# The middle stretch of an attention kernel: its 256-column score step first of four instead of third

## What is computed

```python
xn = _layer_norm(x, ln_g, ln_b)                     # x: (4, 1024, 128)
q, k, v = (xn @ w + b).reshape(B, S, 16, 64).transpose(0, 2, 1, 3)
scores = jnp.einsum('bhqd,bhkd->bhqk', q, k) / jnp.sqrt(jnp.float32(64))
mask = jnp.tril(jnp.ones((S, S), bool), k=-1)
scores = jnp.where(mask, NEG_INF, scores)
a = jax.nn.softmax(scores, axis=-1)
h = jnp.einsum('bhqk,bhkd->bhqd', a, v)
return h.transpose(0, 2, 1, 3).reshape(B, S, 1024) @ w0 + b0 + residual
# then: router on the first tokens, 8 experts of rank 16, top 2, layer norm, residual
```

## Time and profile before

| what | us |
|---|---|
| three runs | 1078.06 (median), 1075.38, 1082.80 |
| the profiled execution's own time | 1075.12 |
| its span, first to last instruction | 1073.4 |
| PE busy | 999.1, 93% |
| POOL busy | 703.0, 65% |
| DVE busy | 584.1, 54% |
| ACT busy | 536.4, 50% |

### The profile page before, as it was taken

One profiled execution on the slowest core, in us unless ns is written; L12 is line 12 of the kernel. 1 busy time (PEld: TensorE's weight loads), 2 busy tenths in 40 slices (PEclk: granted clock), 3 DMA queues, 4 the chain that ended last, 5 costly groups with the idle time before them and its releaser, 6 DMA issues.

```text
span 1073.4 us, 23006 instructions
## 1 busy us (share of the span) xinstructions
PE 999.1 (93%) x9557; PEld 643.1 (60%) x9557; DVE 584.1 (54%) x996; ACT 536.4 (50%) x735; POOL 703.0 (65%) x503
## 2 busy tenths in 40 slices
PE   3699999999999999999999999999999999999972
PEld 2465666666666665666666566666666666666542
DVE  5655554554456556455646656545554555545354
ACT  4244545554444554654455464555355445454343
POOL 6077666667766767785667768666568766666652
PEclk9899999999999999999999999999999999999995
DMA  3000010001101100002010201010100200100101
GB/s 106 20 2 22 21 22 18 6 22 41 22 22 41 22 3 21 22 22 42 21 21 3 61 21 22 22 22 19 25 22 22 61 22 22 22 3 21 22 22 39
DMA packets 61816, 27.11 MB, mean 25 GB/s; under 512 B 39056, under 2 KB 53776, under 8 KB 61712
## 3 DMA queue, kind: packets, MB, share of 16 engines
q1 hardware_dynamic: 61712, 25.64, 10.3%
HBM read 22.76 MB, written 2.35 MB: 23 GB/s over the span
## 4 chain that ended last, share of the span: by engine, by line
PE 81%; DVE 8%; ACT 8%; issue 2%; POOL 1%; DMA 0%; POOLq 0%; ACTq 0%
PE both L614 23%; PE st L599 15%; PE s_ps L560 8%; PE st L653 5%; PE st L594 5%; DVE least L987 4%; PE st L526 4%; ACT ring L835 3%; PE st L588 3%; ACT total L835 3%; PE both L624 3%; PE st L528 3%; PE st L527 3%; PE s_ps L564 2%; PE st L542 2%
## 5 line engine op out<-in xcount | busy, mean ns | idle before, releaser
L407 POOL TENSOR_TENSOR total<-total,ring 128x1024 f32<-128x1024 f32 (+1 forms) x315 | 543.4, 1725 | 317.0 <-PE both L614 268.7
L987 DVE TENSOR_REDUCE least<-s_ps 128x2 f32<-128x1024 f32 x315 | 313.0, 1011 | 280.0 <-PE s_ps L564 185.9
L835 ACT ACTIVATE ring<-st 128x1024 f32<-128x1024 f32 (+1 forms) x256 | 233.7, 918 | 207.2 <-PE st L599 206.8
L614 PE MATMUL both<-ring,v_sb 128*64 128x512 f32 (+3 forms) x1280 | 210.7, 467 | 0.0
L599 PE MATMUL st<-q_high,k_low 64*128 64x512 f32 (+3 forms) x768 | 172.6, 446 | 0.0
L614 PEld LDWEIGHTS both<-ring,v_sb 128*64 128x64 f32 x1280 | 89.0, 137 | 132.9 <-issue 122.9
L560 PE MATMUL s_ps<-k_high,q_high 64*128 64x512 f32 (+1 forms) x758 | 147.6, 402 | 17.5 <-DVE least L987 13.6
L599 PE MATMUL st<-q_high,k_high 64*128 64x512 f32 (+3 forms) x768 | 132.5, 342 | 0.0
L599 PE MATMUL st<-q_low,k_high 64*128 64x512 f32 (+3 forms) x768 | 132.4, 341 | 0.0
L594 PE MATMUL st<-shift_row,pick 64*128 64x128 bf16 (+3 forms) x1152 | 116.0, 271 | 0.5 <-ACT v_sb L869 0.3
L560 PEld LDWEIGHTS s_ps<-k_high,q_high 64*128 64x128 f32 x758 | 71.7, 186 | 72.1 <-issue 36.0
(11 more groups left out here) (151 smaller groups left out, 1284.8 us busy)
## 6 DMA issues: line engine op xcount, KB each, us to landing
inv_row<-sums_dram SPq DMA_DIRECT2D x62, 256.0 KB, 4.1
x_a<-x SPq DMA_DIRECT2D x4, 512.0 KB, 5.3
sums<-sums_row SPq DMA_DIRECT2D x124, 2.0 KB, 2.1
x_b<-x SPq DMA_DIRECT2D x3, 512.0 KB, 5.9
out<-res_b SPq DMA_DIRECT2D x3, 512.0 KB, 4.8
ring<-w_pairs SPq DMA_DIRECT2D x1, 1152.0 KB, 7.0
shift_row<-shift_t SPq DMA_DIRECT2D x64, 4.0 KB
x_a<-x SPq DMA_DIRECT2D x2, 256.0 KB, 3.0
```

Source lines behind the costliest of these rows:

```text
L407: nc.gpsimd.tensor_tensor(so_far, so_far, tile_of(n, s)[:, :, col:col + w], ALU.add).then_inc(s_add, 1)
L614: last = nc.tensor.matmul(po[h * D:(h + 1) * D, 0:w], v_sb[(n // 2) % 2][:, j, c0:c0 + D], tile_of(n, s)[:, h, col:col + w], start=(s in F ...
L835: nc.scalar.activation(tile_of(n, s)[:, :, 0:w], st[s % 2][:, :, 0:w], ACT.Exp, scale=SCALE).then_inc(s_exp, 1)
L987: last = nc.vector.tensor_reduce(least[:, :, a:a + 1], bank[:, :, col:col + w], AX.X, ALU.max, negate=True)
```

## The change

One row of the table `TILES` is reordered. The entry with 256 columns, which was step 5, becomes step 3, and the two entries with 512 columns, which were steps 3 and 4, become steps 4 and 5. Step 6 and the other stretches are as they were, and so is `ORDER`.

```diff
     TILES = [[(0, 7, 512, 0)], [(0, 6, 512, 0)], [(0, 5, 512, 0)],
-             [(0, 4, 512, 0)], [(0, 3, 512, 0)], [(0, 1, 256, 0)], [(0, 2, 384, 0), (0, 0, 128, 384)],
+             [(0, 1, 256, 0)], [(0, 4, 512, 0)], [(0, 3, 512, 0)], [(0, 2, 384, 0), (0, 0, 128, 384)],
              [(1, 7, 512, 0)], [(1, 5, 256, 0)], [(1, 6, 384, 0), (1, 4, 128, 384)]]
```

## The result

Over 22 runs of each, the changed kernel takes 1074.26 us at the median (1067.89 to 1076.60), the kernel before 1079.18 (1075.38 to 1082.80).

The account below looks back on a forecast made before the run. PE, busy for 93% of the span, was taken as the bound. 31 x 0.23 + 0.4 = 7.5 us off 1075.1 gives 1067.6, placed higher at 1069.0 for the median's base; range 1064.5 to 1076.

Parts of the forecast that it names:

- The hole and its size: Middle stretch: T6 waits for T4's exponential; closing this is worth up to 0.28 us a slot, 8.7 us over 31.
- S7's load: Middle stretch: S7's weight load waits for S6's maximum and is partly exposed, 0.04 to 0.13 us late, taken as 0.05.
- Rival 1: S7's weight load is hidden wholly; T6 2.96 us behind T3, 9.1 us gained, 1066 us; chance 0.25.
- Rival 2: The hole ahead of T6 moves rather than closes; T6 3.2 us behind T3, 2 us gained, 1073; chance 0.20.
- What is late next: After S7: S8 is not held by S7's maximum; the fill of k's wait for T5's exponential is hidden by 0.7 us.
- one sign that was to show it: In the profile after, PEld's idle time ahead of T6 for ACT is gone, all but the last slot's.
- POOL and DVE: POOL's adds sum to the same time; `shifts` comes earlier by 2.38 against 1.28 us, then waits for the maxima.
- None of that costs: Claim that the later waits, the shifted last exponential and POOL's reordered adds add no time.
- The sum: Whole kernel: 31 slots x 0.23 us plus 0.4 us in the last slot, 7.5 us gained.
- The base: Profiled execution, 1075.1 us, with the forecast placed half of its 2.9 us difference to the median higher.

Follow-up runs that it names:

- e1: The changed kernel with the 256-column step second of the four instead of first; T3 to T6 3.24 us, ratio to the kernel before 0.9971.
- e4: The changed kernel with S7 issued behind T5 instead of ahead of it; T3 to T6 2.95 us, ratio to the kernel before 0.9995.
- e3: The changed kernel with S6's maximum taken twice, so it comes late; T3 to T6 4.25 us, ratio to the kernel before 1.0263.
- e6: The changed kernel with L972 turned into a negating reduction and L973's constant added on POOL; ratio to the kernel before 0.9898.
- e2: The kernel before with S6's maximum taken twice, so it comes late; T3 to T6 3.85 us, ratio to the kernel before 1.0133.
- e7: The changed kernel with the fill of the softmax's sum issued ahead of S5, slots 1 to 29; ratio to the kernel before 0.9832.

## Why the prediction was right, point by point

**The hole and its size.** Right. T6's wait for T4's exponential was a true hole of 0.28 us in each slot. e1 leaves it, in another place; the changed kernel closes it.

**S7's load.** Right, in kind and size. S7's load waits for S6's maximum 31 times, 0.19 to 0.21 us each, and starts 0.05 us behind it; the pair is up to 0.05 us longer, as e4 confirms against a stretch without it. Rival 1, a wholly hidden load, is out: its 2.96 us is what e4 shows, not what the change shows. Rival 2 is out too, 3.2 was its number.

**What is late next.** Right on PE: neither S8 nor the fill of k gained a wait. DVE's idle time ahead of S7's maximum went from 0.93 to 0.57 us, as forecast by 0.35. Wrong on one sign that was to show it: PEld's idle time ahead of T6 for ACT was to vanish from the list of waits, but 0.28 us of it still stand there, 8.5 us in 30 waits, though ACT is done 0.22 us earlier. I had taken the label for the cause. The sum didn't use the label; it took the hole from PE's starts.

**POOL and DVE.** Here a step failed: "None of that costs". The order of POOL's adds moves which of DVE's small operations fall under an add. Before, four slots paid 0.6 to 1.1 us, 3.4 together; after, four others pay 0.83, and two of the old ones still 0.2, 3.7 together. The net is 0.3 us, so the sum hardly felt it, but that was luck: I had looked at the ends of POOL's work, not at what it blocks while it runs. With it the account closes: 30 x 0.23 = 6.9, less 0.3, is 6.6, against 6.67 measured.

**The sum.** 7.5 us from the rows, of which 0.4 in the last slot; there T3 to T6 fell from 3.26 to 2.86, as reckoned. Measured are 6.67 over 30 slots and 7.5 between the quickest executions. By the ratio it is 6.4.

**The base.** The 5.3 us by which 1069.0 missed the median are the weakest step: "I place the forecast half that difference higher". The profiled execution, 1075.1, was as quick as the quickest group of the kernel before, with 6.8 us at half clock at the start, while that kernel's median over 22 runs is 1079.2. From that base the same sum gives 1071.7. The rest, 2.6 us, is how often each kernel fell into which group: 15 of the changed kernel's 22 in its slower two. Whether the change has a part in that isn't shown; nothing ahead of slot 0's middle stretch differs.

## What to carry to other kernels

Where two banks alternate, a step waits for the exponential of the step two ahead, and what hides it is the work in between. A short step between two long ones hides least: it belongs where the bank's last exponential is long done anyway, here at the start of the stretch, and e1 shows that one place further on is worth nothing. Work taken away ahead of a wait on another engine uses up that engine's lead: read the lead first, since e3 turns the gain into a loss once it is gone. And compare periods slot by slot: a stable gain of 0.23 us a slot was blurred in times that the start moves by up to 7 us.

## What the runs showed of the hardware

- A DVE operation on 4 elements a partition (L972), started under a running POOL add, lasted until 0.02 to 0.03 us behind the add's end, so up to 2.2 us instead of 0.17. A reduction in its place never did (40 of 40 within 160 to 166 ns in e6). Not every POOL operation holds it: in the kernel before, L972 took 0.17 us at 414.95, under the power of POOL's L378, which ran for 0.58 us more.
- PE ran at half clock for 6.8 us of the first 60 in the kernel before's profile, for 23.9 in e1's and for 30.7 in the changed kernel's. S6's maximum of slot 0 came at 59.7, 64.9 and 66.2 us, with the same program up to there. What sets the length wasn't found.
- A matmul pair of 512 columns and 64 rows took 0.23 us in a stream, 0.28 with its load held until 0.07 us ahead of it, 0.35 when PE itself waited and masks followed (S7 in e2), and 0.43 ahead of 128-row matmuls, with a wait or, in e7, without.
